# An edge loop of 98 chunks, written out on all five engines instead of looped

## The reference, cut to what matters

```python
h_fwd, h_rev = h @ W_forward.T, h @ W_reverse.T          # h: layer-normed x, 6250 x 256
messages = h_fwd[src] * direction[:, 0:1] + h_rev[src] * direction[:, 1:2]
scores = leaky_relu(messages @ attn.T, 0.2)
exp_scores = exp(scores - scores.max(axis=0))
sum_exp = segment_sum(exp_scores, dst)
norm = exp_scores / (sum_exp[dst] + 1e-10)
outs = [segment_sum(messages * norm[:, hd:hd + 1], dst) for hd in range(4)]
```

## Time and profile before

| | us |
|---|---|
| three runs | 2499.44, 2498.59, 2497.01 |
| median | 2498.59 |
| the profiled execution | 2504.92 |
| its span, first to last instruction | 2503.1 |

### The profile page before, as it was taken

How to read it: one execution, slowest core, us unless ns; L and a number is a source line. 1 busy time by engine, 2 the same in 40 slices (tenths; PEclk the granted TensorE clock), 3 DMA queues, 4 the chain that set the end, 5 groups by cost and what they waited for, 6 DMA issues and landing times.

```text
span 2503.1 us, 46180 instructions
## 1 busy us (share of the span) xinstructions
PE 2162.4 (86%) x12873; PEld 1868.6 (75%) x12874; DVE 1958.6 (78%) x4609; ACT 357.4 (14%) x1034; POOL 1608.8 (64%) x1725
## 2 busy tenths in 40 slices
PE   7598989899898989999898999999946589999970
PEld 6487878778787877878787787878736478888870
DVE  5797888888788878888888887888848856666657
ACT  4100000000000000000000000000016434444435
POOL 6676767676676767667676766767746753333327
PEclk9699999999999999999999999999955599999995
DMA  6232222222222222223222222222245676666657
GB/s 206 58 69 61 68 61 67 61 67 63 61 67 61 67 60 67 62 61 67 61 67 61 67 63 61 68 61 67 61 133 164 215 215 200 197 199 199 199 168 266
DMA packets 175493, 259.46 MB, mean 104 GB/s; under 512 B 46538, under 2 KB 120479, under 8 KB 174972
## 3 DMA queue, kind: packets, MB, share of 16 engines
q0 software_dynamic: 52672, 119.37, 19.5%
q1 hardware_dynamic: 122556, 136.70, 18.0%
HBM read 218.01 MB, written 38.81 MB: 103 GB/s over the span
## 4 chain that ended last, share of the span: by engine, by line
PE 41%; DVE 31%; issue 16%; DVEq 6%; DMA 3%; SPq 1%; ACT 1%; POOL 1%; ACTq 0%; POOLq 0%
PE p_hot L1007 31%; PE p_win L902 5%; DVE hot_ex L1072 4%; DVE p_hot L1122 4%; DVE p_part L1040 4%; DVE rows L1037 3%; DVEq L1772 3%; DVE onehot L1109 2%; DVE rows L1127 2%; DVE p_y L1995 1%; PE p_y L1940 1%; PE p_h L1930 1%; DVE hid_t L1967 1%; DVE second L1975 1%; DVE back L1980 1%
## 5 line engine op out<-in xcount | busy, mean ns | idle before, releaser
L280 POOL DMA_INDIRECT rows<-node_table,index x1343 | 1278.6, 952 | 506.6 <-issue 398.3
L1007 PE MATMUL p_hot<-parts,onehot 128*128 128x476 f32 x6160 | 1403.5, 388 | 75.7 <-issue 58.0
L1007 PEld LDWEIGHTS p_hot<-parts,onehot 128*128 128x128 f32 x6160 | 1170.8, 192 | 280.9 <-issue 73.5
L1122 DVE SCALAR_TENSOR_TENSOR p_hot<-place_no,place_of_source,p_hot 128x476 f32<-128x476 f32 x440 | 293.1, 711 | 98.9 <-PE p_hot L1007 98.9
L902 PEld LDWEIGHTS p_win<-hot_ex,msg 128*65 128x65 f32 x3136 | 201.8, 143 | 116.6 <-issue 113.3
L902 PE MATMUL p_win<-hot_ex,msg 128*65 128x64 f32 x3136 | 210.9, 227 | 87.4 <-DVE hot_ex L1072 86.3
L956 ACT ACTIVATE p_dve<-score,neg_shift 128x64 f32<-128x64 f32 x98 | 31.2, 318 | 1718.1 <-DVE score L1057 1718.1
L1781 POOL DMA_INDIRECT expert_rows<-ys,back x104 | 102.3, 983 | 269.3 <-DVE ys L2000 146.3
L1109 DVE TENSOR_TENSOR onehot<-key,p_dve 128x896 fp32r<-128x896 f32 x220 | 237.3, 1079 | 36.2 <-PE p_hot L1007 32.9
L1127 DVE TENSOR_REDUCE rows<-p_hot 128x136 f32<-128x952 f32 x220 | 252.8, 1149 | 7.7
L1023 DVE TENSOR_TENSOR shared<-shared,p_win 65x64 f32 x784 | 170.2, 217 | 111.8 <-PE p_win L902 16.0
(11 more groups left out here) (269 smaller groups left out, 1422.2 us busy)
## 6 DMA issues: line engine op xcount, KB each, us to landing
shared<-in_w SPq DMA_DIRECT2D x120, 512.0 KB, 4.5
rows<-node_table,index POOLq DMA_INDIRECT x1343, 3.0
xs<-dispatched SPq DMA_DIRECT2D x104, 129.5 KB, 4.1
shared<-expert_rows SPq DMA_DIRECT2D x12, 896.0 KB, 8.1
key<-hot_keys SPq DMA_DIRECT2D x62, 128.0 KB, 3.0
token_rows<-in_x SPq DMA_DIRECT2D x7, 896.0 KB, 12.8
key<-hot_keys SPq DMA_DIRECT2D x32, 192.0 KB, 3.1
shared<-in_x SPq DMA_DIRECT2D x7, 768.0 KB, 9.1
```

The lines of the kernel that those rows point to most:

```text
L280: pool.indirect_dma_start(out=rows[:, s, k, :], out_offset=None, in_=table, in_offset=bass.IndirectOffsetOnAxis(ap=index[:, s, 0, k:k + 1] ...
L1007: last = pe.matmul(p_hot[:, v, d, 0:PLACES * COLS], onehot[:, v, gr, :], parts[:, gr:NT:GP, m, d * COLS:(d + 1) * COLS], start=(gr == 0 an ...
L1122: last = dve.scalar_tensor_tensor(out=found[:, d], in0=place_no[:, :].unsqueeze(2).broadcast_to([P, PLACES, COLS]), scalar=place[:, ds(f, ...
```

## The change

On each of the five engines the three parts become one: the chunks are written out from the first to the last, and the loop with its 15 turns is gone.

```diff
@@ -844,10 +844,7 @@
                             loaded = begin((b - b % RING, turn))
                         step((b, turn), b % RING, loaded)
 
-                steps(range(begun, RING), None)
-                with eng.Fori(0, TURNS) as turn:
-                    steps(range(RING, RING + BODY), turn)
-                steps(range(LOOPED, NCH), None)
+                steps(range(begun, NCH), None)
```

## The result

| | us |
|---|---|
| after, median of four runs | 2414.24 (2411.67 to 2414.41) |
| before, beside it, median of four | 2499.02 (2497.01 to 2500.71) |
| ratio after to before | 0.9659, interval 0.9642 to 0.9675 |
| after, the profiled execution and its span | 2414.41, 2412.6 |

Built and run once more later, the changed kernel took 2415.02 us (2413.3 to 2417.97), ratio 0.9662 [0.9649 to 0.9676]. The kernel became 3.4% faster.

A forecast was written before the change was run, and what follows sets the result against it. POOL's gathers were taken as the clock, pausing at each jump back for scores delayed by PE's code fetch. Profiled 2504.92 us less 88.4 gave 2416.5; less 6.3 to the median, 2410 us, range 2404 to 2432.

The forecast's parts named there:

- first step: Gather stage loop: without the 14 jumps back POOL's pauses go, 88.4 us, and the stage's end moves along.
- second step: Gather stage: PE and DVE keep up, needing 51.35 us a triple of chunks against POOL's 51.51.
- third step: Written-out chunks on all engines: registers become constants, costed at nothing; POOL's step stays 1.2563 us a gather.
- The fourth: Written-out code on PE and DVE: fetching more code in a straight line costs nothing, at most 41 us.
- The mis-sized term: Whole kernel: the profiled execution lies 6.3 us above the median, so 2416.5 became 2410 us.
- price of 6.3 us a jump: Loop's jump back: POOL's pauses of 88.4 us over 14 jumps, 6.3 us each.
- C: Rival at PE's jump: PE and DVE would stand still there anyway; time stays 2497 to 2499 us; chance 0.03.
- B: Rival in written-out chunks: code fetches add half a microsecond a chunk on PE and DVE, 2451 us; chance 0.08.
- D: Rival at jumps over `If` bodies: they now fetch, 6.1 us each; 2544 us if a quarter do; chance 0.03.
- E: Rival in the expert loop: its 24 PE branches begin to fetch, 94 us come back, 2504 us; chance 0.03.
- a rule and a row differed: PE's loop branch: row 4.14 us, rule some 108 ns, making 14 jumps worth 1.5 us; the row was followed.

## Why the prediction was right

Its first step held: the 14 jumps went, and POOL's pauses with them. Forecast were 88.4 us; POOL's stretch of gathers became 87.3 us shorter, and the end of the stage followed it. In this execution the difference is POOL's step. It was taken unchanged at 1.2563 us and is 1.2573 now, 0.001 us more, which over 1300 gathers is 1.3 us. That is scatter and not the change: in the repeated run the steps are 1.2565 us, and POOL stops once, for 1.4 us.

Its second step held too. Windows of 51.5 us hold 41 gathers each. DVE waits for gathered rows, 20.2 us in 26 waits. They are spread over the stage, 10 of the 26 before 700 us, and do not come late in it, as the forecast had it. The run with the cycle 2, 3 shows how near the other bound is.

The third step, that constants in place of registers are worth nothing, is borne out by the runs with the loop kept: with turns of 12 the fewer and somewhat cheaper jumps account for the whole gain, and the loop with the short `If` body comes within 8 us of the written-out one.

The fourth, nothing for fetching straight-line code, held, against an upper end of 41 us: the pause of DVE between window additions comes 8 times now, from 230 to 1670 us, 0.4 us each, and POOL has no wait there beyond an ordinary gap.

The mis-sized term is the last one, from the profiled execution to the median. The profiled sum was 2416.5, and 2414.4 was measured. But the text took 6.3 us off it, as though an execution of the changed kernel under the profiler would lie above its median as that of before did. It did not (2414.41 against 2414.24). Of the 90.5 us between the spans of the two profiled executions, 3.4 lie ahead of gather 39, a stretch whose length varies from run to run (119.19 us before, 115.77 after, 117.89 in the repeated run). What follows the last gather kept its length, 658.4 us before and 658.6 after. So the median came out at 2414.2 instead of 2410; the gain of 84.8 us has 88.4 within its interval (81.2 to 89.5).

The forecast's price of 6.3 us a jump is right for 14 jumps, but it is no constant: 5.5 us with turns of 12, 0.4 us with the shorter code, nothing with slack on PE.

Of the rivals, C, the jump not being the cost, is refuted by PE alone written out and by the short `If` body. B, PE and DVE falling behind, did not come: POOL shows no pause. D and E did not come either: the jumps over the `If` bodies took 0.37 us at most on PE, those of the expert loop 0.232.

On the branch, where a rule and a row differed, the row was right for this kernel, and the runs say why. The same branch took 0.21 us as soon as the turn's code was short enough. The Trainium skill, page "Runtime: NRT & Kernel Launch", section "Instruction fetch mechanics", says that a taken branch to code outside the fetched window waits until it is brought in. The packets on PE's instruction queue agree: 20 to 22 where the jump takes 0.21 us, 149 and 152 where it takes 4 us.

## What to carry to other kernels

Before a loop is written out, look at what its branch takes on each engine and at that engine's instruction queue: in these runs only a jump that fetched, on an engine without slack, was worth anything. Code that is never entered counts as code, so shortening a body that is jumped over can win nearly as much as writing the loop out (80 of 85 us here). And when a wait goes, work out which engine is next, and by how much: here the next bound lay 0.2 us a triple away, and no shift of work between POOL and PE inside the stage gave more; two sets moved at its very end gave a few microseconds.

## What the runs showed of the hardware that was not expected

The price of PE's jump has two levels, with a step between turns of 720 matmuls (0.21 us) and 776 (4.14 us), counted as the profile counts them and with those that are jumped over; 596 gave 0.21, 912 gave 3.92, and the turns of 12, with 1552, gave 3.74. Where between 720 and 776 the step lies was not tried, nor was the place of the turn's code in memory varied by itself.

With the cycle 2, 2, 2, looped or not, POOL pauses by itself every 112 gathers, twelve times. One of these in the timeline of POOL, in the written-out kernel:

```profile
1350.39 0.95 POOL L280 DMA_INDIRECT rows<-node_table,index  x1 [0.30 <-issue]
1353.52 0.95 POOL L280 DMA_INDIRECT rows<-node_table,index  x1 [2.18 <-issue]
```

These 1.9 us more than a gap, 12 times, are 23 us, and with 32 x 1.257 = 40 us for the added gathers they make the 62.9 us by which POOL's stretch of gathers grew (1701.1 against 1638.2). Gather 39 starts 4.2 us earlier here (111.56 us), so the last one is 58.7 us later. That is why the time rose by 55 us and not by 40. The cause is open; that the looped kernel has them at the same gathers speaks against the layout of the code.

In the kernel after, about every 18 chunks (5 times) rows land some 1 us late and PE stands. PE around one of these:

```profile
1577.33 12.53 PE L1004 MATMUL p_hot<-parts,onehot 128*128 128x476 f32 x56
1592.44 2.54 PE L899 MATMUL p_win<-hot_ex,msg 128*65 128x64 f32 x32 [2.58 <-issue]
1594.83 16.69 PE L1004 MATMUL p_hot<-parts,onehot 128*128 128x476 f32 x70
```

After the 2.58 us the 32 window sums take 2.54 us instead of the 2.08 of other chunks, and the window from 1592 to 1600 us shows a granted clock of 0.79. It costs nothing, since POOL goes on: no wait of its in the stage is longer than 0.3 us. Why the rows are late was not tried.
